# The next block's tokens and first three key loads, issued in the middle of a phase instead of at its boundary

## What is computed

```python
# x: (128, 32, 256); ctx: (128, 257, 256); ln = layernorm over the channels
x = x + cross_attention(ln(x), ctx)      # softmax over 257 keys, then Wo
x = x + mixer(ln(x))                     # selective scan, see below
x = x + ffn(ln(x))                       # 1024 hidden, quantised weights and activations

def mixer(a):
    h = a @ in_w.T + in_b                # 256 -> 512
    u = silu(depthwise_conv3(h))
    d_lr, Bm = split(u @ x_proj_w.T + x_proj_b)      # 64 and 16
    delta = softplus(d_lr @ dt_w.T + dt_b)
    # state s: 512 channels x 16 states, over the 32 tokens of a sequence
    # s = exp(delta * A) * s + delta * u * B ;  y = sum over states of s
    return (y + u * D) @ out_w.T + out_b
```

## Time and profile before

| | us |
|---|---|
| three runs | 1158.01, 1156.97, 1152.78 |
| median | 1156.97 |
| the profiled execution, its own time | 1154.96 |
| its span, from the first to the last instruction | 1153.1 |
| mean granted TensorE clock in it | 0.93 of 2.4 GHz |
| load of x: from issue to landing, median of 7 | 7.8 |
| load of a t part of the keys: from issue to landing, median | 6.5 |

### The profile page before, as it was taken

One profiled execution on the slowest core, in us unless ns is written; L12 is line 12 of the kernel. 1 busy time (PEld: TensorE's weight loads), 2 busy tenths in 40 slices (PEclk: granted clock), 3 DMA queues, 4 the chain that ended last, 5 costly groups with the idle time before them and its releaser, 6 DMA issues.

```text
span 1153.1 us, 12823 instructions
## 1 busy us (share of the span) xinstructions
PE 967.5 (84%) x4042; PEld 499.1 (43%) x4042; DVE 926.1 (80%) x1284; ACT 722.4 (63%) x1291; POOL 859.1 (75%) x617
## 2 busy tenths in 40 slices
PE   6866498899988998989898998889898998776845
PEld 4342244344534453444544453545444454432333
DVE  2312497989998899879997899789997999899935
ACT  2214464687667775867676767777676767765524
POOL 0610799898888897888887888788878888899700
PEclk9567598999999999989998999989998999989977
DMA  8501450344017310453017400632036401400010
GB/s 333 183 19 70 205 184 19 129 194 154 3 54 274 123 61 19 176 201 119 19 51 260 170 15 20 245 140 110 19 111 237 147 18 38 147 1 0 3 35 19
DMA packets 22060, 124.71 MB, mean 108 GB/s; under 512 B 3496, under 2 KB 4136, under 8 KB 9449
## 3 DMA queue, kind: packets, MB, share of 16 engines
q1 hardware_dynamic: 16376, 89.09, 20.8%
q10 hardware_dynamic: 5616, 34.81, 8.1%
HBM read 115.23 MB, written 8.65 MB: 107 GB/s over the span
## 4 chain that ended last, share of the span: by engine, by line
PE 35%; DVE 27%; ACT 13%; issue 11%; POOL 6%; DMA 6%; SPq 1%; ACTq 0%; DVEq 0%; POOLq 0%
PE bank L985 21%; DVE state L860 12%; PE acc L985 9%; DMA x_in<-in_x 3%; POOL state L578 3%; ACT decay L643 3%; ACT soft L629 3%; DVE raw L843 2%; DVE sg L904 2%; DVE u L970 1%; DVE hm L917 1%; ACT hid L660 1%; POOL rstd L541 1%; DVE u L977 1%; PE bank L1103 1%
## 5 line engine op out<-in xcount | busy, mean ns | idle before, releaser
L578 POOL TENSOR_TENSOR state<-w,brep 128x512 f32<-128x512 f32 (+1 forms) x352 | 613.2, 1770 | 41.3 <-PE acc L985 34.8
L860 DVE TENSOR_TENSOR_SCAN state<-decay,state 128x512 f32<-128x512 f32 (+1 forms) x352 | 587.1, 1693 | 45.6 <-POOL state L578 25.7
L985 PE MATMUL acc<-state,ident 128*128 128x512 f32 x832 | 409.9, 608 | 25.7 <-DVE state L860 23.9
L643 ACT ACTIVATE decay<-delta,neg_a 128x496 f32<-128x496 f32 x512 | 328.9, 669 | 99.7 <-DVE state L860 99.0
L985 PEld LDWEIGHTS acc<-state,ident 128*128 128x128 f32 x832 | 148.0, 192 | 183.3 <-issue 113.2
L586 POOL TENSOR_TENSOR state<-state 128x512 f32<-128x512 f32 x96 | 122.6, 1277 | 39.4 <-DVE state L860 39.3
L629 ACT ACTIVATE soft<-x_in,nmr,rstd 128x256 f32<-128x256 f32 x64 | 33.2, 589 | 87.0 <-POOL nmr L544 87.0
L985 PE MATMUL bank<-xn_t,in_w 128*128 128x512 f32 x128 | 68.5, 663 | 22.9 <-DVE u L977 14.8
L609 POOL TENSOR_TENSOR w<-delta,u 128x512 f32<-128x512 f32 x32 | 40.0, 1275 | 46.2 <-ACT delta L768 46.2
L538 POOL TENSOR_TENSOR ve<-mv,eps 128x4 f32<-128x4 f32 x24 | 4.9, 203 | 81.6 <-DVE mv L847 81.6
L985 PE MATMUL bank<-out_w,u 128*128 128x256 f32 x256 | 57.4, 382 | 6.7 <-DVE u L851 6.7
(11 more groups left out here) (138 smaller groups left out, 1354.7 us busy)
## 6 DMA issues: line engine op xcount, KB each, us to landing
keys<-in_keys_t SPq DMA_DIRECT2D x32, 1028.0 KB, 6.5
keys<-in_keys_n SPq DMA_DIRECT2D x32, 1024.0 KB
brep<-b_scratch ACTq DMA_DIRECT2D x32, 1024.0 KB, 6.7
x_scratch<-x_in SPq DMA_DIRECT2D x8, 512.0 KB, 2.6
res<-x_scratch SPq DMA_DIRECT2D x8, 512.0 KB, 5.3
out<-res SPq DMA_DIRECT2D x8, 512.0 KB, 3.1
x_in<-in_x SPq DMA_DIRECT2D x7, 512.0 KB, 7.8
brep<-in_w_gateT SPq DMA_DIRECT2D x1, 1024.0 KB, 12.5
```

The costliest lines, as they stand in the source:

```text
L578: nc.gpsimd.tensor_tensor(state[state_buffer(odd, g)][:, 0:count, :], w[:, m, :].unsqueeze(1).to_broadcast((P, count, TOK)), brep[:, n:n + ...
L643: last = nc.scalar.activation(decay[:, to + i, :, 1:LEN], d, ACT.Exp, scale=neg_a[:, m, n + i:n + i + 1])
L860: nc.vector.tensor_tensor_scan(flat, decay[:, of:of + count, :, :].rearrange("p c q l -> p (c q l)"), flat, 0.0, ALU.mult, ALU.add).then_i ...
L985: return nc.tensor.matmul(o, l, r, start=first, stop=last)
```

## The change

`load_keys` gets the block as an argument, and the loads that a phase needs at its start are issued by the phase before. Behind its own eight key loads, phase j waits for the stored x1 of block j-1 (which had the buffer `x_in[1 - par]`), issues x of block j+1, and then the first three key loads of block j+1. Each of these waits for the last use of its buffer in block j: t0 for the third `attend` (n2 had the buffer), t1 for the fourth (n3), n0 for the fourth `score` (t3). In the queue they now stand ahead of the stores of x1, of B and of `out`, and the next phase begins with the load of `res`. Phase 0 loads its own first three before the weights, as it did. The arithmetic is unchanged.

```diff
             def phase(j, par, pre, scan, post):
-                def load_keys(k):
-                    if k < 3:
-                        reach(sp, z_done, j, 0)
-                    else:
-                        kind, g = KEY_LOADS[k - 3]
-                        reach(sp, scores_done if kind == "t" else z_done, j, g + 1)
+                def load_keys(block_, k):
+
+                    kind, g = KEY_LOADS[k - 3 if k >= 3 else max(range(k, len(KEY_LOADS), 3))]
+                    reach(sp, scores_done if kind == "t" else z_done, block_ - (k < 3), g + 1)
                     kind, g = KEY_LOADS[k]
...
-                if pre and scan:
-                    reach(sp, x1_stored, j - 2, 16)
-                    sp.dma_start(x_in[par][:, :, :], t["x"][j]).then_inc(x_loaded, 16)
                 if post:
                     reach(sp, out_stored, j - 2, 0)
                     sp.dma_start(res[:, :, :], t["x1_scratch"][j - 2]).then_inc(res_loaded, 16)
                 if pre:
-                    for k in range(3):
-                        load_keys(k)
                     if not scan:
+                        for k in range(3):
+                            load_keys(j, k)
                         load_mixer_weights()
                         load_ffn_weights()
                     for k in range(3, len(KEY_LOADS)):
-                        load_keys(k)
+                        load_keys(j, k)
+                    if j + 1 < BLOCKS:
+
+                        reach(sp, x1_stored, j - 1, 16)
+                        sp.dma_start(x_in[1 - par][:, :, :], t["x"][j + 1]).then_inc(x_loaded, 16)
+                        for k in range(3):
+                            load_keys(j + 1, k)
                     reach(sp, res_biased[1], j, 1)
                     sp.dma_start(t["x1_scratch"][j], x_in[par][:, :, :]).then_inc(x1_stored, 16)
```

More of the change, by code:

```diff
@@ L476, in phase @@
             def phase(j, par, pre, scan, post):
-                def load_keys(k):
-                    if k < 3:
-                        reach(sp, z_done, j, 0)
-                    else:
-                        kind, g = KEY_LOADS[k - 3]
-                        reach(sp, scores_done if kind == "t" else z_done, j, g + 1)
+                def load_keys(block_, k):
+                    kind, g = KEY_LOADS[k - 3 if k >= 3 else max(range(k, len(KEY_LOADS), 3))]
+                    reach(sp, scores_done if kind == "t" else z_done, block_ - (k < 3), g + 1)
                     kind, g = KEY_LOADS[k]
                     if kind == "t":
-                        sp.dma_start(keys_t[g], t["keys_t"][j * GROUPS + g]).then_inc(keys_t_loaded[g % 2], 16)
+                        sp.dma_start(keys_t[g], t["keys_t"][block_ * GROUPS + g]).then_inc(keys_t_loaded[g % 2], 16)
                     else:
-                        sp.dma_start(keys_n[g], t["keys_n"][j * GROUPS + g]).then_inc(keys_n_loaded[g % 2], 16)
-                        if j == 0:
+                        sp.dma_start(keys_n[g], t["keys_n"][block_ * GROUPS + g]).then_inc(keys_n_loaded[g % 2], 16)
+                        if block_ == 0:
                             sp.wait_ge(prep_p, PREP_P)
-                        sp.dma_start(keys_l[g % 2][0:GSEQ, :], t["keys_l"][j * GROUPS + g])\
+                        sp.dma_start(keys_l[g % 2][0:GSEQ, :], t["keys_l"][block_ * GROUPS + g])\
                             .then_inc(keys_n_loaded[g % 2], 16)
-                if pre and scan:
-                    reach(sp, x1_stored, j - 2, 16)
-                    sp.dma_start(x_in[par][:, :, :], t["x"][j]).then_inc(x_loaded, 16)
                 if post:
```

## The result

The changed kernel took 1124.63 us (median of four runs, 1116.27 to 1127.42) against 1154.88 (four runs, 1149.06 to 1158.01): a ratio of 0.973, 95% interval 0.967 to 0.980. It is faster by 30 us. The forecast was 1121.5, range 1115 to 1133. The profiled execution took 1125.2, its span fell from 1153.1 to 1123.4 us.

The account below looks back on a forecast made before the run. No engine was full; a mesh of small dependences bound the kernel, the late load of x standing out. Gains of 28.3 + 6.0 = 34.3 us from 1154.96 gave 1120.7, put at 1121.5 us, range 1115 to 1133.

Parts of the forecast that it names:

- What bounds the kernel, and the boundary without a stall as the measure: No engine full; late x stalls five boundaries, each costing 5.59 us against the boundary into phase 2, which has no stall.
- x, 28.3 us: Boundaries into phases 3 to 7: issuing x earlier removes the stall and the slow matmuls behind it, gaining 28.3 us.
- 603.45 as the floor: Five phases as short as phase 2 (120.69 us) would take 603.45 us, against 633.15 for phases 3 to 7 before.
- rival 1: Clock stays slow without the stall: transposes and query matmuls slow at five boundaries, 12.9 us lost, 1134.4 us; chance 0.11.
- Boundary into phase 1, 6.0 us: GpSimd no longer waits for `brep` loads sharing DMA engines with x and three key loads: gain 6.0 us, 3.75 to 6.45.
- The keys at no cost: Next block's three key loads, moved into a 39.9 us stretch with no other load, need some 20 us and cost nothing.
- Rival 4: Key loads delay the store of B, so GpSimd stands in phases 0 to 6; 10 us late gives 1191; chance 0.02.
- `res` next in line: Behind the store of `out`, `res` is late next: at most 0.7 us wait before `x2` per boundary, none expected.
- rival 2: `res` takes the place of x: a wait before `x2`, 0.7 us at five boundaries, 1125 us; chance 0.08.
- Where phases 0, 8 and 9 were costed at nothing: Phases 8 and 9 load no x: zero; phase 0's moved loads fall where nothing is queued.
- The sum: Gains of 28.3 and 6.0 make 34.3 us off the profiled 1154.96, so 1120.7; forecast put at 1121.5.

## Why the prediction was right

*What bounds the kernel, and the boundary without a stall as the measure.* Right: phase 2 of the old trace was the new phase, to 0.1 us (120.69 there; 120.70 and 120.71 in the unslowed phases after).

*x, 28.3 us.* The mechanism was right: the place in the queue (the experiment with x one place ahead of `out`), half of it standing and half the clock (three useless products). The size came out at 24.9. What failed in the term is the assumption that slow `mix_in` groups stay as they were, one in five phases: there were three, 1.65, 1.40 and 1.68 us, 4.7 together against 1.4 before. The 3.4 us more and the 24.9 are the 28.3 of the forecast, and with 603.45 as the floor, 608.24 is those three to 0.1 us. The rule of the Trainium skill ("TensorE: Matmul & The Clock Gate", Part 1), that the clock's switching is not tied to the program, was weighed at the wrong place: the slow query matmuls all left with the stall, so rival 1 was wrong by 12.9 us, but a group behind another thin stretch of TensorE took some of it back, with the same 1.07 us of idle time directly before it whether it was slow or fast. Here the traces agree with it in part only: the same phases, 4, 5 and 7, were slow in four of the five profiles of kernels that had lost the stall and had the gap in the middle (phases 4, 5 and 6 in the one with the keys twice). So it is not chance from run to run alone.

*Boundary into phase 1, 6.0 us.* Measured 6.8 in the first pair of profiles, a little above the bound of 6.45 that I had called the high end. Both waits went whole. The rest, 0.3 us, is within what the stretch does by itself: it took 110.41 to 111.27 us in four profiles with the code of before, and 104.50, 106.71, 104.51 and 104.01 in four with x and the keys both early. The means differ by 5.8. So 6.0 was right, and 6.8 is a single pair.

*The keys at no cost.* Right, and with much room: twice the loads cost nothing. Rival 4 had its deciding point well beyond.

*`res` next in line.* Issued 3.2 us behind `out` at four of the five boundaries, 4.6 at one; no wait before `x2` in phases 3 to 7. Of rival 2 there was a single wait of 0.18 us where the keys stayed behind `res`, and 0.21 and 0.41 us where they were loaded twice.

*Where phases 0, 8 and 9 were costed at nothing*, they differ by +0.90 and +1.07 us. Phase 0's difference was there before the moved loads: its second load of n keys was issued at 37.27 and not 36.10, and the first moved load at 51.14. No run shows it to be an effect of the change. Nor is the +1.07 of the end: that stretch took 162.66 us in the changed kernel with the keys loaded twice, and 163.95 in the kernel before with three useless products, against 162.54 and 163.61 in the pair.

*The sum.* 34.3 was forecast, the spans differ by 29.7 and the medians by 30.2. Some luck is in the closeness of 1121.5 to 1124.63. The forecast took the gain off one profiled execution, with nothing said of phase 0, which varies by 9 us; the two profiled executions both had the long phase 0 (108.5 and 109.4), so it cancelled. Where the changed kernel was run again, phase 0 took 102.5 in its profile, and the ratio of 0.970 is some 35 us. The stretches, not the medians, are what bears out the terms.

## What to carry to other kernels

A load that a stage needs at its start should not stand in a queue behind a wait for the stage before: the place just ahead of that wait gave here all that a place sixty microseconds earlier gives. Where a trace has one boundary with a stall and one without, subtract them aligned on a common instruction: it prices the stall with its consequences (28.3 us), of which the waits alone (15.6 us) show little more than half. And where TensorE's idle time falls before dependent matmuls, ask for the clock as well as for the wait; a few products that nobody reads, no longer than the gap, bought 13 us before the change (11.6 of them in the profile of the five phases) and 7 after it; with products longer than the gap the times showed no gain.

## What was not expected

The time of this kernel varies by 1%, and the granted clock goes with it: the changed kernel ran at 0.950 of the full clock in 1115.93 us and at 0.931 in 1129.72. Much of it is in phase 0, by the stretches and the clock above. What sets the clock there was not tried out.

The slow groups in the middle have no rule that the runs give. At phases of 120.7 us there were three in five, in the same three phases in four of five profiles, although phase 0 had been up to 9 us shorter. With x late there was one in five in two profiles (phase 3, in the kernel before and with the keys alone early), but three in the one with only phase 0's part of the change (3, 6 and 7), at phases of 126 to 128 us. So the length of a phase does not settle how many there are, and whether the change caused the two more is open. What decides it was not tried out; that a single product of 0.9 us in the gap of 1.35 us before the transposes leaves none in phases 2 to 7 is shown, in two kernels and three profiles.
